# One block for normalisation, edge preparation and first GAT layer: rows centred and multiplied tile by tile

## The reference

```python
h = jnp.maximum(_layernorm(x, axis=-1), 0.0)          # (x - m) / sqrt(v + 1e-5)
h1 = (h @ W1).reshape(N, 4, 512)
al_s = jnp.einsum('nhc,hc->nh', h1, a_src); al_d = jnp.einsum('nhc,hc->nh', h1, a_dst)
e = jax.nn.leaky_relu(al_s[src] + al_d[dst], 0.2)
alpha = softmax of e over the edges of one dst
out = segment_sum(h1[src] * alpha, dst)
```

## Time and profile before

| | us |
|---|---|
| median of three runs (1276.36 to 1279.97) | 1278.28 |
| profiled execution | 1277.69 |
| its span | 1275.6 |
| TensorE busy | 1164.8 (91%) |
| TensorE weight loads, beside it | 1073.1 (84%) |
| VectorE busy | 899.4 (71%) |
| ScalarE busy | 520.3 (41%) |
| GpSimd busy | 31.9 (2%) |

### The profile page before, as it was taken

How to read it: one execution, slowest core, us unless ns; L and a number is a source line. 1 busy time by engine, 2 the same in 40 slices (tenths; PEclk the granted TensorE clock), 3 DMA queues, 4 the chain that set the end, 5 groups by cost and what they waited for, 6 DMA issues and landing times. The chain is left out here.

```text
span 1275.6 us, 19953 instructions
## 1 busy us (share of the span) xinstructions
PE 1164.8 (91%) x7118; PEld 1073.1 (84%) x7118; DVE 899.4 (71%) x1877; ACT 520.3 (41%) x1090; POOL 31.9 (2%) x36
## 2 busy tenths in 40 slices
PE   2699998999899999999999999973999999999998
PEld 2477676767789899989998999973999999889998
DVE  7797888986797688768885877867967741351254
ACT  1322222231655575447644775415453732251111
POOL 7000000000200000000000000000000000000000
PEclk9999999999999999999999999996999999999999
DMA  5012130300110111011100210002201220010221
GB/s 197 14 47 90 39 104 33 110 18 1 58 50 1 52 32 51 1 34 50 50 1 20 64 51 1 1 1 75 85 25 51 72 75 1 1 38 1 94 90 59
DMA packets 27634, 58.59 MB, mean 46 GB/s; under 512 B 3493, under 2 KB 6153, under 8 KB 27537
## 3 DMA queue, kind: packets, MB, share of 16 engines
q1 hardware_dynamic: 27344, 56.96, 13.4%
q10 hardware_dynamic: 192, 0.32, 0.1%
HBM read 41.73 MB, written 15.54 MB: 45 GB/s over the span
## 5 line engine op out<-in xcount | busy, mean ns | idle before, releaser
L1202 PE MATMUL banks<-hs,ring_hi 128*128 128x258 f32 (+1 forms) x1600 | 300.3, 288 | 4.0 <-DVE ring_lo L470 2.1
L1202 PEld LDWEIGHTS banks<-hs,ring_hi 128*128 128x128 f32 (+1 forms) x1600 | 248.7, 189 | 5.7 <-issue 2.5
L1202 PE MATMUL banks<-hs,ring_lo 128*128 128x258 f32 (+1 forms) x800 | 227.1, 284 | 0.0
L444 ACT ACTIVATE e<-banks,al 128x256 f32<-128x256 f32 (+1 forms) x500 | 194.5, 492 | 22.3 <-PE banks L429 22.3
L1202 PEld LDWEIGHTS banks<-hs,ring_lo 128*128 128x128 f32 (+1 forms) x800 | 151.0, 189 | 0.0
L452 ACT ACTIVATE ring_hi<-pf 128x512 fp32r<-128x512 f32 (+1 forms) x125 | 81.7, 654 | 156.0 <-DVE pf L463 152.9
L1230 PE MATMUL banks<-w_hi,oT_hi 128*128 128x384 f32 (+1 forms) x320 | 109.0, 341 | 12.6 <-DVE rows L944 6.9
L793 DVE TENSOR_SCALAR hot<-iota,key 125x320 uint16 x488 | 114.7, 301 | 0.2
L461 DVE TENSOR_TENSOR e<-e 128x512 f32<-128x512 f32 (+1 forms) x125 | 84.6, 677 | 39.2 <-ACT e L444 39.0
L1230 PE MATMUL banks<-w_lo,oT_hi 128*128 128x384 f32 (+1 forms) x320 | 108.3, 339 | 0.0
L1230 PE MATMUL banks<-w_hi,oT_lo 128*128 128x384 f32 (+1 forms) x320 | 108.3, 338 | 0.0
(11 more groups left out here) (241 smaller groups left out, 2223.0 us busy)
## 6 DMA issues: line engine op xcount, KB each, us to landing
h_scratch<-stage SPq DMA_DIRECT2D x30, 256.0 KB, 2.0
hs<-h_scratch SPq DMA_DIRECT2D x30, 256.0 KB, 2.9
w_st<-in_L_gnn_W SPq DMA_DIRECT2D x4, 1536.0 KB, 9.8
w_st<-in_L_gnn_W SPq DMA_DIRECT2D x16, 384.0 KB, 3.4
gw_st<-in_L_gnn_W SPq DMA_DIRECT2D x12, 384.0 KB, 3.9
xr<-in_x SPq DMA_DIRECT2D x9, 384.0 KB, 6.8
rows<-in_x SPq DMA_DIRECT2D x9, 384.0 KB, 3.4
x_scratch<-rows SPq DMA_DIRECT2D x9, 384.0 KB
```

The costliest lines, as they stand in the source:

```text
L444: last = nc.scalar.activation(self.e[:, local % 2, a, i, 0:n], self.p_shift[:, a, 0:n], ACT.Exp, bias=scores[a][:, g * G + i:g * G + i + 1])
L1202: last = nc.tensor.matmul(p_a[0:m, dt, half, 0:HH], wt.ring[a][:, s // G, s % G, dt * P:dt * P + m], hs[:, s, b, half * HH:(half + 1) * HH ...
```

## The change

`front` is gone as a block; its work stands in `first_layer`. Rows are no longer normalised before they are turned. VectorE takes a tile's mean (`x_mean`), ScalarE subtracts it (`centre`, Identity with a bias), the tile is turned and clipped, and projected without the deviation; rstd is multiplied in when the product leaves PSUM: `stage`, `hs` high and low, and `al`. This holds since rstd is positive, so that it can be taken out of the clipping. Root chains are made for tiles 0 to 2, 3 to 5 and 6 to 9. Pairs of tiles alternate with projection tiles 0 to 4. The windows come behind tiles 5 to 28 (EDGES = 5). The weights of the first head are loaded behind two tiles of x, its vectors last; the next head's at n = 9 instead of 6. The loads of the window words have bounds (min_val, max_val). New names ER, RS generalise the edge layout; with ER = EJ = 4 they give RS = 1, EP = NS = 80 as before. Tiles of x, stats and edge buffers lie in other memory.

```diff
+ER = 4
+EP = NCH // ER
 EJ = 4
+RS = ER // EJ
-EP = NS
+EDGES = T // 2
...
     def windows_after(n):
 
-        return range(n * NW // (FIRST - 1), (n + 1) * NW // (FIRST - 1)) if n < FIRST - 1 else range(0)
+        span, i = FIRST - 1 - EDGES, n - EDGES
+        return range(i * NW // span, (i + 1) * NW // span) if 0 <= i < span else range(0)
...
-        return [engine.value_load(bounds[0:1, wd:wd + 1]) for wd in range(first, min(NW, first + count))]
+        return [engine.value_load(bounds[0:1, wd:wd + 1], min_val=0, max_val=((NW + 1) * NS << 16) - 1)
+                for wd in range(first, min(NW, first + count))]
...
         def _(sp):
+            for t in range(T):
+                if t == T - 1:
+                    sp.wait_ge(pad_zero, 1)
+                sp.dma_start(xr[t][0:rows_of(t), :], x[t * P:t * P + rows_of(t), :]).then_inc(tile_in[t], 16)
+                if t == 1:
+                    load_weights(sp, 0)
+            load_vectors(sp, 0)
             for n in range(FIRST):
                 i = n // T
-                if n in (6, 16, 22):
-                    j = {6: 1, 16: 2, 22: 3}[n]
+                if n in (9, 16, 22):
+                    j = {9: 1, 16: 2, 22: 3}[n]
                     sp.wait_ge(v_done, 2 * KD * j)
                     sp.wait_ge(wlo_done, KD * j)
+                    load_vectors(sp, j)
                     load_weights(sp, j)
...
-            for t in range(T):
-                nc.gpsimd.tensor_scalar(xr[:, t, :], xr[:, t, :], rstd[:, t:t + 1], nmr[:, t:t + 1],
-                                        ALU.mult, ALU.add).then_inc(h_done, 1)
...
+            def centre(t):
+                act.wait_ge(mean_ready, t + 1)
+                nc.scalar.activation(xr[t][:, :], xr[t][:, :], ACT.Identity, bias=nmean[:, t:t + 1]).then_inc(centred, 1)
+
+            def x_hi(t):
+                act.wait_ge(xt_done, t + 1)
+                nc.scalar.activation(xT[0][:, :, t * P:(t + 1) * P], p_x[t % 2][:, 0:KD, :], ACT.Relu).then_inc(hi_done, 1)
...
-                nc.scalar.activation(stage[:, n % 2, :], p_h[n % 2], ACT.Copy).then_inc(h_out, 1)
+                if n < T:
+                    act.wait_ge(rstd_ready, 1 + (n >= ROOTS[1][0]) + (n >= ROOTS[2][0]))
+                nc.scalar.activation(stage[:, n % 2, :], p_h[n % 2], ACT.Copy, scale=rstd[:, n % T:n % T + 1]).then_inc(h_out, 1)
+
+            centre(0)
+            centre(1)
+            x_hi(0)
+            weight_hi(0)
+            x_hi(1)
+            for j in range(1, T // 2):
+                for t in (2 * j, 2 * j + 1):
+                    centre(t)
+                    if t in LAST_ROOT:
+                        take_root(LAST_ROOT.index(t))
+                for t in (2 * j, 2 * j + 1):
+                    x_hi(t)
+                spill(j - 1)
+            for n in range(T // 2 - 1, FIRST):
...
+                if n == EDGES:
+                    act.wait_ge(bounds_ready, 1)
...
+            def x_mean(t):
+                dve.wait_ge(tile_in[t], 16)
+                for k in range(2):
+                    front_step(nc.vector.bn_stats(stats[:, t, k, :], xr[t][:, k * HALF:(k + 1) * HALF]), k == 1)
+                front_step(nc.vector.bn_aggr(mv[:, t, :], stats[:, t, :, :].rearrange("p k s -> p (k s)")))
+                nc.vector.tensor_scalar(nmean[:, t:t + 1], mv[:, t, 0:1], -1.0, None, ALU.mult).then_inc(mean_ready, 1)
...
+            edges_in()
+            x_mean(0)
+            x_mean(1)
+            x_lo(0)
             weight_lo(0)
+            x_lo(1)
+            for j in range(1, T // 2):
+                for t in (2 * j, 2 * j + 1):
+                    x_mean(t)
+                    if t in LAST_ROOT:
+                        variances(LAST_ROOT.index(t))
+                for b in range(len(ROOTS)):
+                    if LAST_ROOT[b] // 2 == j:
+                        inverse(b)
+                if j == 4:
+                    window_bounds()
+                for t in (2 * j, 2 * j + 1):
+                    x_lo(t)
+                if j == 1:
+                    span_ends()
+                if j == 2:
+                    span_windows()
+                    edge_keys()
+            pack_bounds()
+            dve.wait_ge(bounds_ready, 1)
+            dve.wait_ge(keys_done, 1)
+            dve.wait_ge(made, 13)
             for n in range(FIRST):
                 for wd in windows_after(n):
                     count_hot(wd)
...
-                nc.vector.tensor_tensor(hs[:, t, 1, 0:HID], p_h[n % 2], hs[:, t, 0, 0:HID].bitcast(fp32), ALU.subtract).then_inc(hlo_done, 1)
+                nc.vector.scalar_tensor_tensor(out=hs[:, t, 1, 0:HID], in0=p_h[n % 2], scalar=rstd[:, t:t + 1],
+                                               in1=hs[:, t, 0, 0:HID].bitcast(fp32), op0=ALU.mult, op1=ALU.subtract).then_inc(hlo_done, 1)
...
+            pe.wait_ge(made, 9)
+            transpose_edges()
+            turn_x(0)
+            turn_x(1)
             for n in range(FIRST):
+                if n < T:
+                    pe.wait_ge(lo_done, n + 1)
                 tile(n)
+                if n == 3:
+                    transpose_spans()
+                if n + 1 < T // 2:
+                    turn_x(2 * n + 2)
+                    turn_x(2 * n + 3)
+                if n == 3:
+                    window_rows()
+                if n == EDGES:
+                    pe.wait_ge(bounds_ready, 1)
                 for wd in windows_after(n):
                     count(wd)
```

More of the change, by code:

```diff
@@ L91, in __init__ @@
         self.pick = own("pick", [4 * T, 2 * T], f32r)
+        self.at_counts = own.at
         self.counts = own("counts", [P, T, NP], u16)
@@ L668, in count_out, with take_root, spill @@
                                      p_c[wd % 2][:, 0:WK].rearrange("p (d s) -> p s d", s=T), ACT.Copy).then_inc(win_out, 1)
-            weight_hi(0)
-            for n in range(FIRST):
-                if n % T == T - 1:
-                    weight_hi(n // T + 1)
+            act.dma_start(e_i[:, 0, :, :], src.rearrange("(p j e) -> p j e", j=ER, e=EC)).then_inc(e_in, 16)
+            act.dma_start(e_i[:, 1, :, :], dst.rearrange("(p j e) -> p j e", j=ER, e=EC)).then_inc(e_in, 16)
+            def centre(t):
[4 more added lines that the diff above has]
+                nc.scalar.activation(xT[0][:, :, t * P:(t + 1) * P], p_x[t % 2][:, 0:KD, :], ACT.Relu).then_inc(hi_done, 1)
+            def take_root(b):
+                tiles = slice(ROOTS[b][0], ROOTS[b][-1] + 1)
+                act.wait_ge(var_done, b + 1)
+                nc.scalar.activation(root[:, tiles], ve[:, tiles], ACT.Sqrt).then_inc(roots, 1)
+            def spill(n):
                 if n >= 2:
@@ L686, in row_hi @@
                 act.wait_ge(h_ready, n + 1)
-                nc.scalar.activation(hs[:, t, 0, 0:HID], p_h[n % 2], ACT.Copy).then_inc(hhi_done, 1)
+                nc.scalar.activation(hs[:, t, 0, 0:HID], p_h[n % 2], ACT.Copy, scale=rstd[:, t:t + 1]).then_inc(hhi_done, 1)
             for i, (d0, n) in enumerate(SPANS):
@@ new lines, in x_lo, with variances @@
+            def x_lo(t):
+                dve.wait_ge(hi_done, t + 1)
+                nc.vector.scalar_tensor_tensor(out=xT[1][:, :, t * P:(t + 1) * P], in0=p_x[t % 2][:, 0:KD, :], scalar=0.0,
+                                               in1=xT[0][:, :, t * P:(t + 1) * P].bitcast(fp32),
+                                               op0=ALU.max, op1=ALU.subtract).then_inc(lo_done, 1)
+            def variances(b):
+                tiles = slice(ROOTS[b][0], ROOTS[b][-1] + 1)
+                nc.vector.tensor_scalar(ve[:, tiles], mv[:, tiles, 1], EPS, None, ALU.add).then_inc(var_done, 1)
@@ new lines, in inverse @@
+            def inverse(b):
+                tiles = slice(ROOTS[b][0], ROOTS[b][-1] + 1)
+                dve.wait_ge(roots, b + 1)
+                v, r, y, half = ve[:, tiles], root[:, tiles], rstd[:, tiles], tmp[:, tiles]
+                front_step(nc.vector.reciprocal(y, r))
+                front_step(nc.vector.tensor_tensor(half, y, y, ALU.mult))
+                front_step(nc.vector.tensor_tensor(half, half, v, ALU.mult))
+                front_step(nc.vector.tensor_scalar(half, half, -0.5, 1.5, ALU.mult, ALU.add))
+                nc.vector.tensor_tensor(y, y, half, ALU.mult).then_inc(rstd_ready, 1)
@@ new lines, in span_windows @@
+            def span_windows():
+                for r in range(RS):
+                    front_step(nc.vector.tensor_scalar(ov[:, r, :], w_f[:, 0, :], dmm[:, 1, r:r + 1], None, ALU.is_le), r == RS - 1)
+                for r in range(RS):
+                    front_step(nc.vector.scalar_tensor_tensor(out=ov[:, r, :], in0=w_f[:, 1, :], scalar=dmm[:, 0, r:r + 1], in1=ov[:, r, :],
+                                                              op0=ALU.is_ge, op1=ALU.mult), r == RS - 1)
+                for r in range(RS):
+                    for a in range(2):
```

(1 more changed line is left out.)

329 lines of the change are left out of this document (136 added, 193 removed).

## The result

| | before | after |
|---|---|---|
| median, us (four runs each) | 1277.58 | 1304.93 |
| lowest to highest | 1276.36 to 1279.97 | 1303.12 to 1305.3 |
| profiled execution | 1277.69 | 1303.12 |
| its span | 1275.6 | 1301.4 |
| last eviction of `stage` starts | 265.9 | 285.5 |

The changed kernel is slower: the ratio of the times is 1.0209, interval 1.019 to 1.0227, or 27.4 us. The prediction had said 1291.0, with a range of 1279 to 1300. Its sign and most of its mechanism came true; the time lies outside the range.

The account below looks back on a forecast made before the run. VectorE and TensorE were taken as critical by turns, with VectorE having nothing to give. Its first span at 67.2 plus 208.4 put its last column at 275.6 and tile 29's end at 278.0, +12.7: 1278.3 + 12.7 = 1291.0, range 1279 to 1300.

Parts of the forecast that it names:

- First product: Front: TensorE's first projection product comes near 14 us instead of 46.6, a gain of 32 if TensorE alone mattered.
- The cast: Start of VectorE's stream: casting the edges takes 0.7 us (an estimate), after VectorE begins at 7.0.
- Front, the rest: Front on VectorE: 47.8 us of work plus 6.5 of waits from 7.0, so window words asked for at 61.3.
- The root wait in the second pair: Front, second pair of tiles: one more activation table load, 1.3 us (an estimate), on top of VectorE's waits.
- the drain of 1.38 us: ScalarE table switch by the skill's rule: second pair waits some 1.4 us longer, total 1292; no row shows it.
- Checks: Window-word loads with bounds: 0.28 us more per word, 2.8 per batch, +11.2 for four batches on VectorE (8 to 12.8).
- the rival in which the checks hide: Checks hidden behind queued compares or not emitted: tile 29 ends at 266.8, time 1279.8, give or take 3; chance 0.17.
- Weights of head 1: Count stage: load moved from n = 6 to n = 9, so VectorE ends window 7 at 98.0 and waits 5.8 us.
- TensorE bound: Rival for the count stage: TensorE sets the pace and its 32 us arrive, time 1249; chance 0.04.
- Dearer stalls: Rival: TensorE stalls 2 us more per batch of words, head 1's wait is 8, time 1299 to 1303; chance 0.09.
- Evictions with rstd: Copy with a scale by rstd at evictions: costed at nothing; 0.1 us each, up to 4, if uncovered.
- All behind is unchanged: After projection tile 29's end nothing changes, so the whole loss is +12.7 us at that tile's end, 278.0 against 265.3.

Follow-up runs that it names:

- the run with the one line changed: Kernel before with bounds put on the loads of window words, nothing else of the change: 1296.34 us, ratio 1.0122.
- with the maximum in it: Kernel before with a maximum with 80 on the value that is waited on, nothing else: 1282.91 us, ratio 1.0031.
- with the words unchecked: Changed kernel with window words loaded without bounds and a maximum on the awaited value: 1291.85 us, ratio 1.0108.
- with all three edits: Changed kernel with words unchecked (maximum instead), long iotas held behind the cast, head 1's weights at n = 6: 1275.71 us, ratio 0.9965.
- with the columns moved: Changed kernel, words unchecked, iotas behind cast, weights at n = 6, plus head 0's attention columns moved into VectorE's front waits: 1272.08 us, ratio 0.9947.
- with two products: Changed kernel with the third product left out in the 30 projection tiles before the last head: 1296.72 us, ratio 1.0129.
- that with two edits: Changed kernel with words unchecked (maximum instead) and long iotas held behind the cast: 1283.63 us, ratio 1.003.

## Why the prediction was right in kind and too small

**First product.** Forecast near 14. TensorE's timeline, and its longest wait for hot rows:

```profile
20.51 0.76 PE L1096 MATMUL banks<-w_hi,xT_hi 128*128 128x512 f32 x1 [1.22 <-DVE w_lo L670]
...
74.58 0.70 PE L1113 MATMUL banks<-hot 125*128 x2 [9.58 <-DVE hot L687]
```

It comes at 20.5, and the time in between is the cast's: with the iota behind the cast it comes at 13.66.

**The cast: the step that failed.** The prediction put "the edges' cast of 0.7 (an estimate too)" at 7.0. The duration was right for a cast with GpSimd quiet and wrong for one at 6.4. GpSimd's long iota was in the trace of before, and the prediction said of it only that the "iotas end before they are wanted". It asked when the iota's result is needed and not what else its running touches. The move of the cast from 20 to 6.4 put the two side by side. This is 7.0 of the 6.9 us by which the mark missed (19.6 against 12.7); the small terms below cancel. The cast alone would have left the time near 1298, inside the range; it takes the second term that was wrong, the 6.2 us behind the mark, to go beyond 1300.

The Trainium skill, page "SBUF — State Buffer", section "Who interferes with whom", states the rule: VectorE and GpSimd share one pair of ports, a VectorE copy or cast in a two-port mode contends with GpSimd for it, and whichever issues first has it for its whole instruction while the other is blocked. The runs agree: 7.64 with the iota ahead, 0.68 with the iota held back until the cast is done, 0.78 with the iota cut up, and there a piece of the iota takes 0.88 instead of 0.39 behind the cast. That the cast runs in a two-port mode no trace says; it is inferred from its rate. Rows show as well which instructions were in reach of it. The cast moves 1000 elements of each partition in 0.67 us, about 1.5 per ns; the statistics move 768 in 1.00 to 1.02, under 0.8 per ns, and they were not held beside the iota: in the kernel before, every pair takes 1.02, from the first at 5.05 to those behind 13.5, where that iota ends. The same page says that an instruction with one input outside the two-port modes does not contend, which is what these rows show.

**Front, the rest.** The end of VectorE's stream was forecast at 61.3 and came at 66.93. Without the cast's 7.0 it would have been 59.9, 1.4 early. Busy time and waits were each off and cancelled: between 13.90 and 73.00 VectorE was busy for 42.93 us, with the cast's 0.67 that is 43.6 against 47.8 forecast, and it waited 59.10 - 42.93 - 6.06 = 10.1 against 6.5. Of the 4.2 too many, 0.7 is a slip: the 34.83 up to 46.6 already holds the first 0.7 of the weights' low halves (from 45.89), which are added once more. The root wait in the second pair, for which the prediction had added 1.3 for a table load, is the 1.10 at 28.12, hardly more than the 1.02 of the two root waits behind it. ScalarE's timeline:

```profile
26.59 1.28 ACT L543 ACT_TABLE_LOAD   x1
27.89 0.20 ACT L543 ACTIVATE norm_root<-norm_ve 128x3 f32<-128x3 f32 x1
```

Part of the load ran while VectorE was still busy, and the root starts 0.02 behind it: the drain of 1.38 us that the prediction quotes does not show here.

**Checks.** Forecast 2.8 per batch and 11.2 in all. Measured gaps 6.06, 5.96, 6.31 and 5.87, 24.2, against 12.95 before: 11.25. The lines by source for the first batch:

```profile
L406 DVEq TENSOR_LOAD <-bounds x10: 297/304/566, 65.8 to 71.8; - x10
...
L406 DVEq FUSED_REGOPS  x10: 183/183/206, 66.3 to 72.2; - x10
L406 DVEq SEQ_ASSERT  x10: 23/23/35, 66.6 to 72.4; - x10
```

Ten loads from 65.8 to 71.8 are 0.67 apart, against 0.37 in the earlier trace rows. The estimate from the one checked load at line 1794 held: 183 + 23 ns on VectorE where that row, of TensorE's queue, had 170 + 28. VectorE's last column ran until 66.93, so its queue was 1.1 us ahead here, and the rival in which the checks hide is refuted by the gaps and by the run with the one line changed.

**Weights of head 1.** Forecast a wait of 5.8; it was 6.61 (7.09 in the second execution). That the wait for head 2 would vanish was right.

**TensorE bound.** Refuted, by 30.5 us of waits for hot rows and by the run with a third of the products left out.

**Dearer stalls.** This rival's time, 1299 to 1303, is near what was measured, but not for its reason: it wanted 2 us more per batch and a wait of 8 for the weights, and both came as the forecast had them.

**Evictions with rstd.** Costed at nothing, if ScalarE idles before each. Their median went from 598 to 688 ns. The prediction quoted 93 ns per pointer operand from the Trainium skill ("ScalarE: Activation LUTs", "What ACT_TABLE_LOAD costs"); these rows give 90. No run separates the cost of these from the rest; the three stalls leave no room for one on the path.

**"All behind is unchanged": the second term that was wrong.** From the mark to the end the span was 1009.7 before and is 1015.9 now, 6.2 longer, with the same instructions. The two executions differ in the clock granted to TensorE. Two of the ten stretches of 100 us behind the mark, the kernel before:

```profile
365.90:465.90 100.00, 95.53 (x694) 93.76 (x693) 77.51 (x128) 55.83 (x129) 0.00 (x0) 1.00 0.09 27
...
865.90:965.90 100.00, 83.37 (x445) 78.94 (x446) 78.97 (x145) 52.07 (x119) 0.97 (x4) 0.88 0.20 67
```

and the changed kernel:

```profile
385.50:485.50 100.00, 95.52 (x682) 93.75 (x681) 75.51 (x125) 53.46 (x123) 0.00 (x0) 0.98 0.09 28
...
885.50:985.50 100.00, 79.21 (x421) 74.66 (x420) 78.84 (x143) 48.09 (x109) 0.97 (x4) 0.86 0.19 62
```

In the same work the mean clock is 1.00 and 0.88 in one and 0.98 and 0.86 in the other. Short stretches at the lower of the two levels, 1.2 GHz, make up the shortfall: over the ten stretches it adds up to 0.17 of 100 us before and 0.25 after, and as the lower level is half the higher, that is 34 and 50 us at 1.2 GHz. Each of the 16 us more goes with about 0.4 us of length. The other profiles fit: 0.27 (54 us) in the second profile of the changed kernel, 8.1 longer than before, and 0.34 (68 us) in the kernel before with checked words, 12.1 longer. No run holds the clock fixed, so that the clock is the whole of the 6.2 is argued from these rows and not shown. The part behind the mark was between 1009 and 1011 in the profiles of the kernel before, with the maximum in it, with the words unchecked, with all three edits, with the columns moved and with two products, and between 1014 and 1022 in the others. It is no fixed property of a kernel: that with two edits was profiled at 1290.13 with 1017.9 behind its mark, while its fastest execution, 1280.85, leaves room for about 1009. The kernel before itself ran between 1275.65 and 1287.59 over these sessions. But none of the eight executions of the changed kernel was below 1302.59, so the part behind the mark was near 1015 or longer each time (an estimate for the six that were not profiled, from the mark and the 1.7 us outside the span), and the change seems to bring these stretches with it. Whether its longer idle times in the count stage lead to them was not settled, and I leave it open.

**Sum.** At the mark: 12.7 forecast, 7.0 for the cast, -0.1 for the rest, 19.6. Behind it 6.2 in the profiled pair, less 0.4 outside the spans (1.7 against 2.1 us): 25.4, the difference of the two profiled executions. The medians stand 1.8 above and 0.1 below these, which makes 27.4.

## What to carry to other kernels

When an instruction is moved in time, look at what runs on the neighbour engine at its new place, not only at what waits for what: one copy beside a long GpSimd instruction cost ten times its length, and holding that instruction back or cutting it up gives it back. A checked load of a register is queue time of every engine that makes it, and where that engine sets the pace it is paid; forty words at 0.3 us were 11 us of gaps, and 9.0 and 13.3 us at the mark in the two kernels where they were tried. When a reordering that ought to gain loses, undo its side effects one at a time before giving it up: here three small edits turned 2% slower into 0.35% faster, and a fourth into 0.5%.

## What the hardware did that I had not expected

- A cast from int32 to fp32 on VectorE, 0.67 us alone, took 7.64, 7.34 and 7.38 us in three traces because a GpSimd iota that reads no tensor was under way; it ended 0.5 us after the iota. In the five traces of the changed kernel that have this order it ended at 14.01, whether it had begun at 6.36 or at 7.07. With the iota in forty instructions it took 0.78, and the piece of the iota behind it took 0.88 instead of 0.39.
- One kernel's executions spread over up to 12 us (before: 1275.65 to 1287.59) with the granted clock between 0.968 and 0.985 on the mean. Below some 5 us a difference here can't be read from one execution; the mark at tile 29 can, for it moved by 0.4 us between the two executions of the changed kernel.
